# A graph network on one core: GpSimd gathers rows during the recurrent passes, VectorE takes over the low parts, five row buffers, another middle split

## The chip, the core and the metric

The kernel runs on one core of a Trainium2 chip. The metric is the device time of one execution in microseconds; lower is better. The engines are named TensorE (PE, its weight loads PEld), VectorE (DVE), ScalarE (ACT), GpSimd (POOL) and SyncE (SP) as in the profile.

## The reference

Four graph layers follow one another on 6250 nodes of 128 features and 100000 edges, each behind a layer norm and ReLU and with a residual sum. What matters here:

```
edge_index = [src, dst];  agg(h) = segment_sum(h[src], dst, 6250)

x = x + L0(h)   # three times: h = h + agg(h); two dense layers with batch norm and ReLU
x = x + L1(h)   # messages weighed by a sigmoid of source and target scores,
                # summed by target, one GRU step, batch norm over the nodes
x = x + L2(h)   # encoder; then five times:
                #   agg = segment_sum((h @ conv_w[i])[src], dst)
                #   r, z, n gates of a GRU on agg and h; h = (1 - z) * n + z * h
                # then relu, decoder of two dense layers, sigmoid
x = x + L3(h)   # segment_sum(h[src], dst) @ W.T + b
return x
```

## The kernel before

The edges are sorted and turned into a matrix of counts, `count` (6272 by 6272, one byte each) in HBM. Every segment sum is then a dense product of the states with the counts. 6272 rows are 49 blocks (`NB`) of 128. The product is done in thirds of the target columns: per third the whole of 49 blocks `k` is run through, and its sums stand in up to five PSUM banks (`SUMS`). The thirds have 10, 8 and 7 pairs of blocks (`THIRD_PAIRS`), so 2560, 2048 and 1792 columns. A pass over the graph is three thirds, 147 blocks.

`Flow.run` writes out a pipeline over blocks `g` by hand, one program for each engine, tied by semaphores. There are two flows. The first has 8 thirds of plain sums (392 blocks) and an attention part; the second has six layers (18 thirds, 882 blocks): five GRU steps, the last of them with the decoder behind it (`Decode`), and the last graph layer (`Out`). In the second flow third 13, the middle one of layer 4, is blocks 637 to 685, and third 16, the middle one of the last layer, is blocks 784 to 832. For block `g`:

- SyncE loads the counts of the block into one of `row_slots` buffers (9 in the first flow, 6 in the second), once the block that lay there has been widened by both engines. Behind the load may stand four DMAs that put shuffled states of a chunk in place (line 2110).
- VectorE cuts the high part off the state block (`high`, line 2571) and widens the right part of the byte counts to float32r (`wide`, line 2065 is the helper `widen` for both engines). ScalarE makes `hi` of `high` (line 2435) and widens the columns below `BY_ACT[q]`: 1024, 768 and 768 for the three thirds.
- GpSimd subtracts: `lo` = state - `high` (line 2164). For blocks from 3 on this waits until `used` says that TensorE has finished block `g - 3`, thus `used >= g - 2`.
- TensorE multiplies `hi` and `lo` with `wide`, bank by bank (line 2226). It waits for `hi`, `lo` and ScalarE's part, and for VectorE's part only before the first bank that needs it. At the end of a block it counts `used` up. `high`, `hi`, `lo` and `wide` have three buffers each.

The chunks (one or two blocks of finished sums) of the third before are worked off in between, one every four blocks: gate products, sigmoids and tanh, the GRU update on VectorE, the shuffle. Chunks of the decode layer go through a longer chain, at fixed distances in blocks from their start (`CHAIN`): hidden 5, decoded 7, relu 8, biased 10, opened 11, scaled 12, kept 14, bias 17. The first decode chunk starts at block 638, so its inverse root stands at block 650 of GpSimd's program (lines 2127 to 2177, it counts `scaled` up), and its normalization at step 652 of ScalarE's (line 2537):

```
for c in self.due(g - CHAIN["kept"], "decode"):
    u = c.late % 2
    e.wait_ge(s["scaled"], c.late)
```

VectorE waits at chunk `late` for `scaled` of chunk `late - 2`. Every engine's instructions run in the order of its program, so a wait holds all that stands behind it.

The only indirect DMAs before are ten gathers in the sort (line 443), 128 rows of 1536 bytes each.

Of the kernel before, what the change touches and what calls it, by code (L numbers as in the profile page):

```python
# [9 lines left out]
F32 = mybir.dt.float32  # L10
# [6 lines left out]
I32 = mybir.dt.int32  # L17
# [6 lines left out]
D = 128  # L24
# [34 lines left out]
SUMS = [[(128, 384), (512, 512), (1024, 512), (1536, 512), (2048, 512)],  # L59
        [(0, 512), (512, 512), (1024, 512), (1536, 512)],  # L60
        [(0, 512), (512, 512), (1024, 512), (1536, 256)]]
BY_ACT = [1024, 768, 768]
ROW_BYTES = 10 * PAIR
ROW_SLOTS = 9
STEP_ROW_SLOTS = 6
WIDE_SLOTS = 3
CUT_SLOTS = 3
HEAD = 4
# [95 lines left out]
class Count:  # L164


    def __init__(self, engine, sem):
        self.engine, self.sem, self.n = engine, sem, 0
# [1709 lines left out]
class Flow:  # L1878
# [1 line left out]

    def __init__(self, net, layers, add_self=False, enter=None, given=()):
        self.net, self.layers, self.add_self, self.enter, self.given = net, layers, add_self, enter, given
        self.row_slots = ROW_SLOTS if enter is None else STEP_ROW_SLOTS
        self.gated = isinstance(layers[0], Gru)
        self.kinds = ["dense" if isinstance(l, list) else "leave" if isinstance(l, Leave) else "attend" if isinstance(l, Attend) else "out" if isinstance(l, Out) else "decode" if l.after else "gru"
                      for l in layers]
        self.parts = [(n, q) for n, kind in enumerate(self.kinds) for q in (ATTEND_PARTS if kind == "attend" else range(3))
                      if n or q not in given]  # L1890
        self.total = len(self.parts) * NB
        self.plain = sum(self.kinds[n] != "attend" for n, _ in self.parts) * NB
        self.head, self.chunks = [], []
        self.need = [[0] * NB for _ in layers]
        made = moved = self.products = 0
        ahead = 0 if given else HEAD if enter is None else HEAD + ENTER["source"]
        for q in () if given else range(3):
            for b, n in self.chunk_blocks(q):
                made += 1
                at = b - ahead - (enter is not None and b == 0)  # L1900
                self.head.append(Chunk(b, n, -1, -1, at, -made, 0, 0, at + ahead - HEAD, made, 0))
        for third, (n, q) in [(-1, (0, q)) for q in given] + [*enumerate(self.parts)]:
            base, tail = (third + 1) * NB, third + 1 == len(self.parts)
            moves = n + 1 < len(layers) and self.kinds[n] in ("dense", "gru")
            for j, (b, nb) in enumerate(self.chunk_blocks(q)):
                spaced = 2 if tail else LEAVE_EVERY[q] if self.kinds[n] == "leave" else EVERY
                at = base + (TAKE_AT + 1 if tail else 1) + spaced * j
                made += n + 1 < len(layers) and not moves
                moved += moves
                late = 1 + sum(c.layer == n for c in self.chunks)  # L1910
                turn = late if self.kinds[n] == "attend" else len(self.chunks) + 1
                self.chunks.append(Chunk(b, nb, n, third, at, turn, j % 2 if tail else 0, int(tail and j > 0),
                                         at + LAG, made, late, moved if moves else 0))
        self.starting, self.turning = defaultdict(list), defaultdict(list)
        self.moving = defaultdict(list)
        self.shuffled = {}
        for c in self.chunks:
            self.starting[c.at].append(c)
            if c.moved:
                self.moving[c.at + WIDE_SLOTS + 2].append(c)  # L1920
        for c in self.head + self.chunks:
            if c.layer + 1 < len(layers):
                if c.layer < 0:
                    self.turning[c.product].append(c)
                    self.products = c.made
                for b in range(c.first, c.first + c.blocks):
                    if c.moved:
                        self.shuffled[c.layer + 1, b] = c
                    self.need[c.layer + 1][b] = c.late if c.layer >= 0 and self.kinds[c.layer] == "leave" else c.made
        self.entering = {c.at: c for c in self.head} if enter is not None else {}  # L1930
        self.steps = range(-ahead - 2 * (enter is not None), self.chunks[-1].at + LAG + WIDE_SLOTS + 1)
# [49 lines left out]

    def run(self):
        net, nc, ps = self.net, self.net.nc, self.net.ps
        total, plain, gated, layers = self.total, self.plain, self.gated, self.layers
        L = 0 if gated else len(layers[0])
        final = layers[-1].out if self.kinds[-1] == "out" else None
# [9 lines left out]
            "first", "second", "mid", "gates", "rz", "pre", "new", "next", "dve", "gated", "gate", "weighed", "attended",  # L1996
            "hidden", "relu", "decoded", "biased", "opened", "spread", "pool", "scaled", "biases", "last", "done", "store",
            "measured", "power", "factors", "normal", "turned", "added", "seen", "rooted", "even", "back", "plain",
            "coded", "code", "encoded", "entered", "squares", "moved0", "moved1", "w_turned", "w_cut", "w_made", "w_kept", *[f"lv_{n}" for n in LEAVE if leaving]]
        with ExitStack() as tmp, stage(nc, *names) as (block, s):  # L2000
            wide = scratch(nc, tmp, "wide", [P, WIDE_SLOTS, ROW_BYTES], F32R)
            high = scratch(nc, tmp, "high", [P, CUT_SLOTS, P], I32)
# [12 lines left out]
            ring = net.ring[:, :, :].rearrange("p j f -> p (j f)")  # L2015
            rows = ring[:, 0:row_slots * ROW_BYTES].rearrange("p (j f) -> p j f", f=ROW_BYTES)
            if self.enter is not None:
                c0, size = row_slots * ROW_BYTES, self.enter.steps * 3 * D * 4
                combined = ring[:, c0:c0 + size].bitcast(F32).rearrange("p (n g f) -> p n g f", g=3, f=D)
                turned_w = net.aggT[:, 0:self.enter.steps * D]  # L2020

# [22 lines left out]
            def like(tile, layer, k):  # L2044

                return tile.rearrange("p (i b) -> p i b", b=SQUARE) if (layer, k) in self.shuffled else tile
# [13 lines left out]
            def along(row, n):  # L2060
                return row.rearrange("p (a f) -> p a f", a=1).to_broadcast([P, n, P])
# [61 lines left out]
            def _(e):  # L2123
# [9 lines left out]
                for g in self.steps:  # L2133
# [23 lines left out]
                        e.tensor_scalar(m, m, -1.0, None, ALU.mult).then_inc(s["lv_root"], 1)  # L2157
                    if not 0 <= g < plain:
                        continue
                    n, q, k = self.where(g)  # L2160
                    e.wait_ge(s["high"], g + 1)
                    if g >= CUT_SLOTS:
                        e.wait_ge(s["used"], g - CUT_SLOTS + 1)
                    e.tensor_tensor(like(lo[:, g % CUT_SLOTS, :], n, k), piece(n, k), like(high[:, g % CUT_SLOTS, :].bitcast(F32), n, k),  # L2164
                                    ALU.subtract)\
                        .then_inc(s["lo"], 1)
                    for c in self.due(g - CHAIN["scaled"], "decode"):
                        u = c.late % 2
                        mean, var = (mv[u][:, 0:c.blocks, i] for i in (0, 1))
# [8 lines left out]
                    for c in self.due(g - CHAIN["bias"], "decode"):  # L2178
                        e.wait_ge(s["kept"], c.made)
                        x = net.xN[:, c.cols].rearrange("p (b f) -> p b f", f=P)  # L2180
                        e.tensor_tensor(x, x, along(layers[c.layer].after.next_bias, c.blocks), ALU.add).then_inc(s["biases"], 1)

            @block.tensor
            def _(e):
# [364 lines left out]
            def _(e):  # L2549
                ch = Count(e, s["dve"])  # L2550
                for g in self.steps:
# [9 lines left out]
                    if 0 <= g < plain:  # L2561
                        n, q, k = self.where(g)
                        c = self.shuffled.get((n, k))
                        if c is not None and q == 0:
                            e.wait_ge(s[f"moved{c.moved % 2}"], (c.moved + 1) // 2 * SQUARES * 16)
                        elif q == 0 and self.need[n][k]:
                            e.wait_ge(s["kept"], self.need[n][k])
                        if g >= CUT_SLOTS:
                            e.wait_ge(s["hi"], g - CUT_SLOTS + 1)
                            e.wait_ge(s["lo"], g - CUT_SLOTS + 1)  # L2570
                        e.tensor_scalar(like(high[:, g % CUT_SLOTS, :], n, k), piece(n, k, I32), HIGH_BITS, None, ALU.bitwise_and)\  # L2571
                            .then_inc(s["high"], 1)
                        e.wait_ge(s[f"row{g % row_slots}"], g // row_slots * 16 + 16)
                        if g >= WIDE_SLOTS:
                            e.wait_ge(s["used"], g - WIDE_SLOTS + 1)
                        widen(e.tensor_copy, g, BY_ACT[q], THIRD_PAIRS[q][1] * PAIR).then_inc(s["wide_dve"], 1)
                    if g >= NB and g % NB == TAKE_AT and g // NB <= last_third:
                        take(e, g // NB - 1, self.takes(g // NB - 1)[0], "took_dve")

# [116 lines left out]
def program(nc, a, out):  # L2696
# [3 lines left out]
    with ExitStack() as ctx:  # L2700
# [68 lines left out]
        def wt(key):  # L2769
            return [net.wT[:, i, :] for i in names[key]]  # L2770
# [82 lines left out]
        with ExitStack() as room:  # L2853
# [8 lines left out]
            step, decoded = [Gru(wt("2ih"), wt("2hh"), *gru_biases(b2i, b2h, b2s), after=after)  # L2862
                             for after in (None, Decode((wt("2d1")[0], d1[:, :]), (wt("2d2")[0], d2_row[:, :]), b3_row[:, :]))]
            Flow(net, [step] * (steps - 1) + [decoded, Out(wt("3")[0], out)],
                 enter=Enter(states_bn[:, :], gam[:, :], bet[:, :], encoder, w_steps, steps, wt("2ih"))).run()


        flag = nc.values_load(many[0:1, 0:1], min_val=0, max_val=1)
# [35 lines left out]
```

## Time and profile before

| | us |
|---|---|
| median of 2 runs | 4062.59 (4062.26 to 4062.91) |
| profiled execution | 4062.36 |
| its span in the trace | 4060.0 |
| TensorE, VectorE, ScalarE, GpSimd busy | 3727.4, 3118.8, 2452.0, 1336.7 |

The trace's span is 2.4 us shorter than the time of the same execution. The mean granted clock of TensorE was 0.994 of full speed. Time in the trace counts from the span's start; the second flow's blocks run from 1998 to 4046.5 us. A busy TensorE isn't TensorE at its peak, since matmuls overlap. Idle time on an engine that is not the bottleneck costs nothing.

### The profile page before, as it was taken

The page shows a single profiled execution, that of the slowest core. Times are in us where ns is not written, and L with a number is a line of the kernel's source. Part 1 is how long each engine was busy: PE and PEld are TensorE (multiplying, and loading weights), DVE is VectorE, ACT ScalarE, POOL GpSimd, SP SyncE. Part 2 cuts the span into 40 slices and gives each one's busy share as a digit, 9 for nine tenths or more (in the row PEclk, how much of TensorE's full clock was granted, in tenths as well). Part 3 has the DMA queues.
Part 4 walks back from the last instruction along what each step waited for, and adds up shares of the span by engine and source line. Part 5 has one row for each costly group of instructions (what it writes and reads, how often), then busy time and mean ns, then how long its engine had stood idle before and what let it go on. Part 6 is the DMA issues. An engine that isn't in the chain of part 4 may idle for free.

```text
span 4060.0 us, 59938 instructions
## 1 busy us (share of the span) xinstructions
PE 3727.4 (92%) x17068; PEld 2915.6 (72%) x17068; DVE 3118.8 (77%) x5632; ACT 2452.0 (60%) x4604; POOL 1336.7 (33%) x1931
## 2 busy tenths in 40 slices
PE   0138889999999999999899999999999999999999
PEld 0126678888888644555688888888888888888887
DVE  9999956677687777877668767877876876786685
ACT  1129956656656787787565555555565555566655
POOL 0011145534545310000361343244244234446624
PEclk9999999999999999999899999999999999999999
DMA  2029954545543322221144444444444445434344
GB/s 64 0 102 365 364 179 135 160 136 142 160 125 104 92 72 73 74 62 53 59 114 119 123 136 130 122 136 130 123 132 137 119 117 141 122 100 111 116 134 135
DMA packets 320447, 509.08 MB, mean 125 GB/s; under 512 B 118819, under 2 KB 187164, under 8 KB 319735
## 3 DMA queue, kind: packets, MB, share of 16 engines
q1 hardware_dynamic: 299484, 452.24, 39.0%
q0 software_dynamic: 7696, 46.93, 3.2%
q10 hardware_dynamic: 12938, 6.05, 0.7%
q8 instruction: 143, 2.34, 0.2%
q14 instruction: 186, 1.52, 0.1%
HBM read 396.98 MB, written 43.87 MB: 109 GB/s over the span
## 4 chain that ended last, share of the span: by engine, by line
PE 50%; issue 0%; ACT 0%; DVE 0%; POOL 0%; ACTq 0%; POOLq 0%
PE ps L2226 41%; PE ps L2342 3%; PE ps L2343 3%; PE ps L2345 1%; PE ps L2344 1%; PE ps L2372 0%; PE ps L2258 0%; PE ps L2328 0%; PE ps L2367 0%; PE ps L2264 0%; PE ps L2249 0%; ACT wide L2065 0%; PE ps L2241 0%; PE ps L2383 0%; PE ps L2193 0%
## 5 line engine op out<-in xcount | busy, mean ns | idle before, releaser
L2226 PE MATMUL ps<-wide,hi 128*128 128x512 f32 (+2 forms) x5537 | 2148.5, 390 | 21.2 <-issue 9.6
L2226 PE MATMUL ps<-wide,lo 128*128 128x512 f32 (+2 forms) x5537 | 2075.9, 379 | 0.0
L2065 DVE CAST wide<-ring 128x1536 fp32r<-128x1536 uint8 (+2 forms) x1274 | 1310.7, 1029 | 492.4 <-PE ps L2226 487.9
L2226 PEld LDWEIGHTS ps<-wide,hi 128*128 128x128 f32 x5537 | 1041.9, 188 | 226.2 <-issue 31.0
L2226 PEld LDWEIGHTS ps<-wide,lo 128*128 128x128 f32 x5537 | 1043.1, 188 | 189.1
L2065 ACT CAST wide<-ring 128x768 fp32r<-128x768 uint8 (+1 forms) x1274 | 1153.5, 905 | 3.2 <-DMA ring<-count 2.4
L2435 ACT CAST hi<-high 128x128 fp32r<-128x128 f32 x1274 | 381.3, 299 | 1042.8 <-PE ps L2226 621.8
L2164 POOL TENSOR_TENSOR lo<-hN,high 128x128 fp32r<-128x128 f32 x686 | 563.3, 824 | 754.4 <-PE ps L2226 438.6
L2164 POOL TENSOR_TENSOR lo<-hB,high 128x128 fp32r<-128x128 f32 x588 | 495.4, 843 | 751.2 <-PE ps L2226 492.5
L2222 PE MATMUL ps<-hN,hB 128*128 128x512 f32 (+1 forms) x1274 | 526.2, 570 | 5.6 <-DVE aggT L2398 4.2
L2428 ACT ACTIVATE hN<-aggT,source_scores 128x512 f32<-128x512 f32 (+1 forms) x637 | 428.9, 695 | 119.0 <-PE ps L2222 87.8
L2559 DVE TENSOR_TENSOR hN<-hN,ring 128x512 f32<-128x512 f32 (+1 forms) x637 | 402.4, 668 | 110.5 <-ACT hN L2428 105.5
L2222 PEld LDWEIGHTS ps<-hN,hB 128*128 128x128 f32 x1274 | 241.4, 191 | 264.3 <-issue 209.6
L2571 DVE TENSOR_SCALAR high<-hN 128x128 int32<-128x128 int32 x686 | 225.1, 328 | 8.3 <-DVE hB L2686 3.9
L2587 DVE SCALAR_TENSOR_TENSOR room<-ps,b2h,room 128x256 f32<-128x256 f32 (+1 forms) x125 | 59.9, 479 | 204.2 <-ACT room L2456 204.2
L2571 DVE TENSOR_SCALAR high<-hB 128x128 int32<-128x128 int32 x588 | 197.1, 335 | 0.6 <-POOL lo L2164 0.6
L473 PE MATMUL ps<-ident,aggT 128*128 128x128 f32 x112 | 27.5, 427 | 168.4 <-DVE aggT L191 168.4
L686 ACT ACTIVATE aggT<-ps 128x1024 uint16<-128x1024 f32 x196 | 165.6, 846 | 26.4 <-PE ps L634 26.3
L2343 PE MATMUL ps<-hT,wT 128*128 128x256 f32 (+1 forms) x600 | 175.8, 375 | 0.0
L634 PEld LDWEIGHTS ps<-right,left 128*128 128x128 bf16 x1225 | 99.5, 158 | 97.1 <-DVE left L586 49.4
L2127 POOL TENSOR_SCALAR states_bn<-states_bn 128x1 f32<-128x1 f32 x1 | 0.2, 231 | 506.7 <-POOLq L151 506.7
L634 PE MATMUL ps<-right,left 128*128 128x128 bf16 x1225 | 124.6, 242 | 39.2 <-DVE right L588 38.4
(244 smaller groups left out, 3384.6 us busy)
## 6 DMA issues: line engine op xcount, KB each, us to landing
ring<-count SPq DMA_DIRECT2D x490, 320.0 KB, 3.0
ring<-count SPq DMA_DIRECT2D x441, 256.0 KB, 2.7
ring<-count SPq DMA_DIRECT2D x490, 224.0 KB, 2.6
wide<-aggT POOLq DMA_DIRECT2D x49, 896.0 KB, 6.4
count<-aggT SPq DMA_DIRECT2D x49, 800.0 KB, 4.0
hB<-mid SPq DMA_DIRECT2D x192, 32.0 KB, 1.9
hN<-mid SPq DMA_DIRECT2D x192, 32.0 KB, 1.9
hB<-squares SPq DMA_DIRECT2D x96, 32.0 KB, 2.2
```

The lines of the kernel that those rows point to most:

```text
L634: ins = e.matmul(ps[:, bank + t % PER // 4, t % 4 * P:(t % 4 + 1) * P], left[u][:, :, t], right[u][:, :, t, :], start=True, stop=True)
L686: e.activation(rows[k % ROW_BUFFERS][:, t0 * P:t1 * P], ps[:, bank:bank + 2, :].rearrange("p b f -> p (b f)") [:, 0:(t1 - t0) * P], ACT.Co ...
L2065: return copy(wide[:, g % WIDE_SLOTS, c0:c1].rearrange("p (t u f) -> p t u f", u=2, f=P), rows[:, g % row_slots, c0:c1].rearrange("p (t f ...
L2164: e.tensor_tensor(like(lo[:, g % CUT_SLOTS, :], n, k), piece(n, k), like(high[:, g % CUT_SLOTS, :].bitcast(F32), n, k), ALU.subtract)\
L2222: ins = e.matmul(ps[:, c, 0:size], source(n, k), weights(g, c), start=k == 0, stop=k == NB - 1, skip_group_check=True)
L2226: ins = e.matmul(ps[:, c, 0:size], part[:, g % CUT_SLOTS, :], wide[:, g % WIDE_SLOTS, w0:w0 + size], start=k == 0 and part is hi, stop=k = ...
L2342: e.matmul(o, gates_of(c)[g_], net.aggT[:, c.cols], start=True, stop=False)
L2343: e.matmul(o, gru.w_state[g_], net.hT[:, c.cols], start=False, stop=True)
L2428: e.activation(weights(g, c), layers[n].target_scores[:, sums_at(q, c)], ACT.Sigmoid, bias=layers[n].source_scores[:, k:k + 1]).then_inc(s ...
L2435: e.copy(hi[:, g % CUT_SLOTS, :], high[:, g % CUT_SLOTS, :].bitcast(F32)).then_inc(s["hi"], 1)
L2559: e.tensor_tensor(gate, gate, rows[:, g % row_slots, c0:c1].rearrange("p (t f u) -> p t u f", u=2, f=P), ALU.mult).then_inc(s["weighed"], 1)
L2571: e.tensor_scalar(like(high[:, g % CUT_SLOTS, :], n, k), piece(n, k, I32), HIGH_BITS, None, ALU.bitwise_and)\
```

## The change

`lo` goes from GpSimd to VectorE, behind VectorE's widening, in both flows. The middle third's split goes from 768 to 1024 columns for ScalarE. The second flow has five row buffers; the sixth buffer's bytes become four tiles of 128 by 128 float32 and a list of row numbers. In the second flow GpSimd issues, at the first block of each middle third (blocks 49, 196, 343, 490, 637, 784), 144 indirect DMAs of 128 rows of the input `x` (512 bytes each) into the four tiles in turn; all but the first four of a burst add to what is there. Each waits for the one before it on its tile. Nothing reads the tiles. At its end GpSimd's program waits for all of them.

The four hunks after the constants are the buffers, GpSimd's program at block g, its end, and VectorE's program at block g.

```diff
-BY_ACT = [1024, 768, 768]
+BY_ACT = [1024, 1024, 768]
-STEP_ROW_SLOTS = 6
+STEP_ROW_SLOTS = 5
...
             if self.enter is not None:
-                c0, size = row_slots * ROW_BYTES, self.enter.steps * 3 * D * 4
+                c0, size = (row_slots + 1) * ROW_BYTES, self.enter.steps * 3 * D * 4
+                spare = ring[:, row_slots * ROW_BYTES:(row_slots + 1) * ROW_BYTES].bitcast(F32)
+                tiles = spare[:, 0:4 * D].rearrange("p (n f) -> p n f", f=D)
+                names = spare[:, 4 * D:4 * D + 36].bitcast(U32)
...
-                    n, q, k = self.where(g)
-                    e.wait_ge(s["high"], g + 1)
-                    if g >= CUT_SLOTS:
-                        e.wait_ge(s["used"], g - CUT_SLOTS + 1)
-                    e.tensor_tensor(like(lo[:, g % CUT_SLOTS, :], n, k), piece(n, k), like(high[:, g % CUT_SLOTS, :].bitcast(F32), n, k),
-                                    ALU.subtract)\
-                        .then_inc(s["lo"], 1)
+                    if self.enter is not None and g == NB:
+                        e.iota(spare[:, 4 * D:4 * D + 36].bitcast(I32), pattern=[[29, 36]], base=0, channel_multiplier=41).then_inc(s["named"], 1)
+                        e.wait_ge(s["named"], 1)
+                    if self.enter is not None and g % (3 * NB) == NB:
+                        e.wait_ge(s["used"], g - 1)
+                        for i in range(144):
+                            m = 36 * (g // (3 * NB)) + i // 4
+                            if m:
+                                e.wait_ge(s[f"acc{i % 4}"], 16 * m)
+                            if i < 4:
+                                e.indirect_dma_start(out=tiles[:, i % 4, :], out_offset=None, in_=self.x,
+                                                     in_offset=bass.IndirectOffsetOnAxis(ap=names[:, i // 4:i // 4 + 1], axis=0))\
+                                    .then_inc(s[f"acc{i % 4}"], 16)
+                            else:
+                                e.indirect_dma_start(out=tiles[:, i % 4, :], out_offset=None, in_=self.x,
+                                                     in_offset=bass.IndirectOffsetOnAxis(ap=names[:, i // 4:i // 4 + 1], axis=0), compute_op=ALU.add)\
+                                    .then_inc(s[f"acc{i % 4}"], 16)
...
+                if self.enter is not None:
+                    for j in range(4):
+                        e.wait_ge(s[f"acc{j}"], 16 * 36 * (plain // (3 * NB)))
...
                         if g >= CUT_SLOTS:
                             e.wait_ge(s["hi"], g - CUT_SLOTS + 1)
-                            e.wait_ge(s["lo"], g - CUT_SLOTS + 1)
                         e.tensor_scalar(like(high[:, g % CUT_SLOTS, :], n, k), piece(n, k, I32), HIGH_BITS, None, ALU.bitwise_and)\
                             .then_inc(s["high"], 1)
...
                         widen(e.tensor_copy, g, BY_ACT[q], THIRD_PAIRS[q][1] * PAIR).then_inc(s["wide_dve"], 1)
+                        e.wait_ge(s["high"], g + 1)
+                        e.tensor_tensor(like(lo[:, g % CUT_SLOTS, :], n, k), piece(n, k), like(high[:, g % CUT_SLOTS, :].bitcast(F32), n, k),
+                                        ALU.subtract).then_inc(s["lo"], 1)
```

## Rows read from the trace of the kernel before

**Rows 1.** The page's part 1: busy us, share of the span, instructions

```profile
PE 3727.4 (92%) x17068; PEld 2915.6 (72%) x17068; DVE 3118.8 (77%) x5632; ACT 2452.0 (60%) x4604; POOL 1336.7 (33%) x1931
```

**Rows 2.** Busy time by stretches: us, PE, PEld, DVE, ACT, POOL, clock, DMA

```profile
2118.00:2233.00 115.00, 114.98 (x522) 96.24 (x521) 99.13 (x156) 63.56 (x128) 26.00 (x48) 1.00 0.44 120
2233.00:2340.00 107.00, 107.00 (x514) 90.42 (x513) 80.62 (x160) 64.21 (x132) 43.09 (x53) 1.00 0.45 124
...
3597.00:3730.00 133.00, 126.48 (x609) 106.08 (x608) 94.07 (x234) 84.46 (x185) 78.17 (x156) 0.99 0.36 100
...
3865.00:3960.00 95.00, 94.86 (x438) 78.99 (x437) 83.97 (x112) 51.85 (x100) 22.86 (x50) 1.00 0.48 134
3960.00:4046.50 86.50, 86.50 (x439) 73.06 (x438) 55.60 (x109) 52.22 (x101) 46.80 (x49) 1.00 0.49 142
```

**Rows 3.** Groups of instructions by form, 1400 to 4060 us

```profile
L2065 ACT CAST wide<-ring 128x768 fp32r<-128x768 uint8 x588 | 488.6, 831 | 0.4
...
L2065 DVE CAST wide<-ring 128x1280 fp32r<-128x1280 uint8 x294 | 435.7, 1482 | 28.9 <-PE ps L2226 28.6 <-issue 0.3
...
L2065 ACT CAST wide<-ring 128x1024 fp32r<-128x1024 uint8 x294 | 307.5, 1046 | 0.1
...
L2065 DVE CAST wide<-ring 128x1024 fp32r<-128x1024 uint8 x294 | 203.1, 691 | 82.1 <-PE ps L2226 82.0
```

**Rows 4.** Groups by form, VectorE, counting stage (280 to 520 us)

```profile
L602 DVE TENSOR_TENSOR lo<-hN,high 128x128 fp32r<-128x128 f32 x49 | 14.2, 290 | 3.4 <-PE ps L648 3.4
```

**Rows 5.** Timeline of VectorE, middle third of the first recurrent pass

```profile
2184.91 1.48 DVE L2065 CAST wide<-ring 128x1280 fp32r<-128x1280 uint8 x1
2186.30 0.42 DVE L2595 TENSOR_TENSOR hT<-hT,room 128x256 f32<-128x256 f32 x1
```

**Rows 6.** The view of DMA issues: KB each, us to landing

```profile
ring<-count SPq DMA_DIRECT2D x490, 320.0 KB, 3.0
...
hN<-sorted_keys,tile_i POOLq DMA_INDIRECT x10, 3.1
```

**Rows 7.** Timeline of GpSimd, the sort's ten indirect gathers

```profile
252.22 1.26 POOL L443 DMA_INDIRECT hN<-sorted_keys,tile_i  x1 [248.70 <-DVE tiles_before L364]
...
264.21 1.03 POOL L443 DMA_INDIRECT hN<-sorted_keys,tile_i  x1 [0.30 <-issue]
```

**Rows 8.** Timeline of VectorE beside and after those gathers

```profile
256.83 0.42 DVE L393 TENSOR_SCALAR hN<-hN,flip_col 128x384 int32<-128x384 int32 x1 [0.28 <-DMA hN<-sorted_keys,tile_i]
...
266.66 0.41 DVE L393 TENSOR_SCALAR hN<-hN,flip_col 128x384 int32<-128x384 int32 x1
```

**Rows 9.** Line 2164 (lo) by stretches from the flow's start; x counts blocks

```profile
1997.80:3493.70 1495.90, 531.57 (x638) 1.00 0.46 127
...
1997.80:3868.00 1870.20, 633.97 (x785) 1.00 0.44 124
```

**Rows 10.** Timeline of GpSimd, middle third of the decode pass

```profile
3489.47 1.24 POOL L2164 TENSOR_TENSOR lo<-hN,high 128x128 fp32r<-128x128 f32 x1 [0.94 <-PE ps L2226]
...
3493.83 0.46 POOL L2164 TENSOR_TENSOR lo<-hN,high 128x128 fp32r<-128x128 f32 x1 [1.72 <-PE ps L2226]
...
3525.76 0.23 POOL L2127 TENSOR_SCALAR root<-mv 128x1 f32<-128x1 f32 x1 [1.75 <-DVE mv L2657]
...
3528.59 0.36 POOL L2177 TENSOR_SCALAR off<-off 128x1 f32<-128x1 f32 x1
```

**Rows 11.** Timeline of ScalarE, the same stretch

```profile
3529.15 0.83 ACT L2065 CAST wide<-ring 128x768 fp32r<-128x768 uint8 x1
3529.89 0.49 ACT L2537 ACTIVATE hB<-xN,off,inv 128x128 f32<-128x128 f32 x1
...
3537.01 0.30 ACT L2435 CAST hi<-high 128x128 fp32r<-128x128 f32 x1 [0.90 <-DVE high L2571]
```

**Rows 12.** Timeline of GpSimd, middle third of the last layer

```profile
3868.14 0.46 POOL L2164 TENSOR_TENSOR lo<-hB,high 128x128 fp32r<-128x128 f32 x1 [1.72 <-PE ps L2226]
```

**Rows 13.** Timeline of SyncE's queue at the end

```profile
4048.65 4.67 SPq L2084 DMA_DIRECT2D out<-xN  x8
```

More of the change, by code:

```diff
@@ L1878, with __init__ @@
 class Flow:
-    def __init__(self, net, layers, add_self=False, enter=None, given=()):
+    def __init__(self, net, layers, add_self=False, enter=None, given=(), x=None):
+        self.x = x
         self.net, self.layers, self.add_self, self.enter, self.given = net, layers, add_self, enter, given
@@ L1998, in run @@
             "measured", "power", "factors", "normal", "turned", "added", "seen", "rooted", "even", "back", "plain",
-            "coded", "code", "encoded", "entered", "squares", "moved0", "moved1", "w_turned", "w_cut", "w_made", "w_kept", *[f"lv_{n}" for n in LEAVE if leaving]]
+            "coded", "code", "encoded", "entered", "squares", "named", "acc0", "acc1", "acc2", "acc3", "moved0", "moved1", "w_turned", "w_cut", "w_made", "w_kept", *[f"lv_{n}" for n in LEAVE if leaving]]
         with ExitStack() as tmp, stage(nc, *names) as (block, s):
@@ L2864, in program @@
             Flow(net, [step] * (steps - 1) + [decoded, Out(wt("3")[0], out)],
-                 enter=Enter(states_bn[:, :], gam[:, :], bet[:, :], encoder, w_steps, steps, wt("2ih"))).run()
+                 enter=Enter(states_bn[:, :], gam[:, :], bet[:, :], encoder, w_steps, steps, wt("2ih")), x=a["x"]).run()
         flag = nc.values_load(many[0:1, 0:1], min_val=0, max_val=1)
```

## The prediction

> **What bounds the kernel now.** I read the page's totals first, then stretches of the recurrent flow, then single engines. TensorE is busy 92% of the span, GpSimd 33% [rows 1]. In a recurrent pass (49 blocks in each of three thirds) TensorE is busy 114.98 us of 115 and 107.00 of 107 at full clock, VectorE 99 and 81, GpSimd only 26 and 43 [rows 2]: TensorE bounds five of the six passes and nothing that relieves another engine shortens them. The exception is the stretch with the decode chain: 126.48 of 133 us, so 6.5 us of TensorE idle [rows 2]. The two last thirds (3865 to 4046.5) are TensorE-bound again. So I look for what the change can put *in front of* TensorE, and there GpSimd counts for its place in the program, not for its load.
>
> **VectorE and ScalarE part.** In the middle third VectorE widens 1280 columns in 1482 ns, in the last third 1024 columns in 691 ns [rows 3]. The new middle split leaves it 1024 columns, the very form of the last third: 0.79 us less per middle block. ScalarE goes from 768 to 1024 columns, 831 to 1046 ns [rows 3], 0.22 us more; it is busy 63.56 us of 115 there [rows 2], 74 after, so this costs nothing; without that slack it would be 0.22 us for each of 294 blocks. The subtraction for `lo` took 290 ns as a VectorE instruction of the same form in the counting stage [rows 4], so at most 0.29 us per block, in all 1274 blocks. In the middle third VectorE, busy 99 us of 115, comes to 99 - 49 x (0.79 - 0.29) = 75; the start-to-start time of a 1280-column widening, 1.39 us (2184.91 to 2186.30) [rows 5], is no longer most of a block. In the last third it comes to 81 + 49 x 0.29 = 95 us of 107 [rows 2], still below TensorE. `lo` now comes behind the widening, so TensorE can no longer begin a block on ScalarE's columns alone. VectorE works up to three blocks ahead, which hides it; where a flow starts with nothing ahead it costs at most one widening, 1 us for each of two flows. VectorE's wait for GpSimd's `lo` becomes program order. What can be won is the idle of the decode stretch; of the 6.5 us I take 5, between 0 and 6.5.
>
> **Five row buffers.** A load is now asked for five blocks ahead instead of six. Five of the shortest blocks last over 8 us (86.5/49 = 1.77 us each [rows 2]); row loads land in 3 us [rows 6]. Cost nothing; were it to bite it would show as row waits on ScalarE and VectorE.
>
> **The gathers: length of one burst.** 144 indirect DMAs, issued in order by GpSimd, with at most four under way, since each waits for the one four before it. The nearest rows are ten indirect gathers of 128 rows in the sort: first at 252.22, tenth at 264.21, so 1.332 us from one to the next, of which 1.03 is the instruction and 0.30 the gap in the last one [rows 7]. They land 3.1 us after issue [rows 6]; four slots last 5.3 us, so at that landing time issue is the limit, not the chain. A burst is 144 x 1.332 = 192 us. The sort's rows are 1536 B, these 512 B; the number of rows is the same. Bounds: 144 x 1.03 = 148 us with no gap, and upward what accumulation or contention costs (rivals): some 290 us. Rows speak for little contention: VectorE's one-input operation on 384 columns, two results a cycle, lasts 0.42 us under a gather's issue and 0.41 us with none [rows 8], and the 1.332 us of the train already hold such neighbours. But a widening is longer. In the middle third of the last layer (95/49 = 1.94 us a block [rows 2]) it and the cut take 0.60 + 0.13 us from start to start, 38% of the time. I let a quarter of that fall on the gathers, my choice between none and all: 9%, 210 us for the last burst, and 197 us for the fifth, of which only the first 43 us run beside a busy VectorE.
>
> **Where bursts lie.** They stand at blocks 49, 196, 343, 490, 637 and 784, each released when TensorE has finished two blocks before. In the first four GpSimd owes nobody anything: `lo` has moved away, and a pass, 1495.9/638 x 147 = 345 us [rows 9], is longer than a burst. Price nothing.
>
> The fifth is another matter. The 639th `lo` of the flow, which has the same condition as this burst, starts at 3493.83 [rows 9, 10]. Behind it in GpSimd's program stand the decode's inverse roots, the first at block 650, at 3525.76 and done at 3528.8 [rows 10]. ScalarE in its step 652 waits for `scaled` before it goes on to the next block's `hi` and widening; it widened block 652 at 3529.15 and cuts `hi` of 655, which needs TensorE done with 652, at 3537.01 [rows 11]. So ScalarE sticks, and TensorE runs dry at about 3537. It goes on when the burst has been issued, plus 3.1 us for the roots, 0.5 us for the normalization and 1.1 us for `hi` and widening. Stop = 3493.8 + 197 + 4.7 - 3537 = 159 us. None of it is given back: TensorE is the bound behind it. Bounds: 110 us at 148, 252 us at 290.
>
> The sixth burst starts with the `lo` at 3868.14 [rows 9, 12], later by the stop. The block's GpSimd program ends in a wait for all of it. Issue 210, last landing 2, and the 4 us that lie before between the last store's issue and landing and the span's end (store queue busy 4048.65 to 4053.3 [rows 13], landing some 2.5 us later, my estimate from the landings of rows 6): 3868.1 + 210 + 2 + 4 = 4084 against a span of 4060, so 24 us more; 0 at 148 us, 104 at 290.
>
> **Sum.** 4062.4 (the profiled execution, 0.2 us from the median) - 5 + 159 + 24 = 4240 us, +4.4%.
>
> **Rivals.** (1) *Accumulation is slow.* If a gather that adds takes L from issue to landing, a tile's chain sets the burst: 36 x L, which overtakes issue at L = 5.33 us. For it: the adding form isn't in this trace, and every landing here shares the engines with row loads. Against: 3.1 us leaves 2.2 us of room, and a row is a third as long. At L = 8: 288 us, stop 250, tail 102, 4410 us.
>
> (2) *The shared port.* GpSimd's subtraction grows from 0.46 to 1.24 us beside VectorE's widenings [rows 10], so some exclusion exists. If descriptor writing stood still under each fast widening and cut, the sixth burst would be 192/(1-0.38) = 310 us and the fifth 43 + (192 - 27) = 208: stop 170, tail 124, 4351 us. And if VectorE in turn waited out a whole issue (1 us) before its widening and its cut, a middle block would be 3.7 us instead of 2.47: some 60 us for each of five bursts, 4650 us. Rows 8 speak against both. The Trainium skill, "SBUF — State Buffer", section "Who interferes with whom", states such a lock: a VectorE operation in a two-port mode fully blocks GpSimd's descriptor writes, and by that rule the time would be this rival's 4351. The trace agrees for GpSimd's compute instructions and, in ten gathers, shows next to none of it for issue.
>
> (3) *Issue goes by bytes: not slower.* If issuing 512-byte rows took a third of 1.03 us and the gap vanished beside it, a burst were 49 us, the stop 11 and the tail nothing: 4068 us, within 2%. The point is the burst at which the stop passes 81 us, 120 us, or 0.83 us a gather. Against: nothing in the ten gathers ties the issue to the bytes, which land long after it; the list of rows that GpSimd goes through is as long.
>
> (4) *GpSimd does not gate the decode*, because its waits are laid out otherwise than I read, leaving only the tail: 4081 us. Against: the order in the program, and ScalarE's normalization at 3529.89 that follows the roots' end at 3528.95 [rows 10, 11].
>
> **Chances.** Forecast (both terms, bursts of 180 to 230 us) 0.60; slow accumulation 0.18; port lock 0.14; rivals 3 and 4 0.05; anything else slower 0.03. The range goes from bursts of some 150 us (stop 112, 4170) to those of some 300 (4430). A measurement tells 2%, 81 us, from no change: slower 0.94, same 0.05, faster 0.01.
>
> **What would show it.** GpSimd: 864 indirect DMAs at 1.3 to 1.5 us spacing in six trains. TensorE: no loss in passes one to four, which stay as long as before; one hole of some 160 us in the decode pass, ended by ScalarE, itself released by GpSimd's offsets; an end at which only GpSimd works. VectorE's middle widenings at 0.69 us. I am wrong if the hole isn't there, if passes one to four lengthen (port or row buffers), or if spacing is over 1.7 us.

## The result: 7.8% slower, a 229 us stop and a 98 us tail

The changed kernel takes 4379.48 us (2 runs, 4378.09 to 4380.87) against 4062.59 us: ratio 1.078, 95% interval 1.0765 to 1.080. The profiled execution took 4380.87 us, its span in the trace 4376.2 us, 316.2 us more than before. The page's totals (busy us, share of the span, instructions), the chain that ended last by engine, and GpSimd's costliest group (count, busy us, mean ns, idle time before it):

```profile
PE 3724.4 (85%) x17068; PEld 2916.4 (67%) x17068; DVE 2934.5 (67%) x6906; ACT 2523.5 (58%) x4604; POOL 1731.2 (40%) x1522
...
PE 40%; POOL 11%; issue 3%; ACT 1%; DVE 1%; DMA 0%; ACTq 0%; DVEq 0%; POOLq 0%
...
L2179 POOL DMA_INDIRECT ring<-in_x,ring x840 | 1395.6, 1661 | 258.4 <-issue 255.4
```

TensorE does the same 17068 matmuls in the same busy time as before [rows 1], in a longer span. It has no more work; it has more idle time. GpSimd is busy 40% on the page, which is still no bottleneck by load, yet it now holds 11% of the chain that ended last. Where it does so is seen by stretches (us, then busy PE, PEld, DVE, ACT, POOL, clock, DMA share, GB/s):

```profile
2131.00:2471.00 340.00, 339.34 (x1576) 286.62 (x1575) 235.72 (x600) 203.22 (x376) 242.64 (x145) 1.00 0.69 156
...
3151.00:3491.00 340.00, 339.34 (x1576) 286.68 (x1575) 234.86 (x599) 203.69 (x376) 242.62 (x145) 1.00 0.69 156
3491.00:3533.00 42.00, 41.66 (x195) 34.74 (x193) 25.37 (x73) 23.04 (x43) 35.30 (x23) 1.00 0.62 133
3533.00:3763.00 230.00, 1.57 (x4) 1.31 (x5) 0.91 (x3) 2.67 (x6) 189.10 (x130) 0.51 0.29 35
3763.00:3790.00 27.00, 26.95 (x121) 22.11 (x120) 21.02 (x69) 19.66 (x38) 12.41 (x26) 0.95 0.37 103
...
4266.00:4376.00 110.00, 3.64 (x27) 2.96 (x25) 2.98 (x7) 0.00 (x0) 80.67 (x53) 0.54 0.30 41
```

The first four passes, each with a burst in it, cost next to nothing: TensorE is busy 339.3 us of 340. A busy engine need not be one at its peak, so the length counts too: from ScalarE's first `hi` of block 49 to that of block 637 it is 1360.3 us here (2127.9 to 3488.2) and 1359.8 in the kernel without gathers (2126.8 to 3486.6). From 3533 to 3763 TensorE works 1.57 us of 230, and hardly anything but GpSimd is busy; from 4266 to the end the same. The waits of the stretch 3480 to 3800 (engine, tile and line, released by; us in total, times, longest) name both links of the stop:

```profile
ACT hB L2556 <- POOL off L2192: 236.0, 4, 233.8
...
PE ps L2245 <- ACT wide L2070: 228.8, 1, 228.8
```

One wait of 233.8 us for GpSimd's offsets, and behind it one of 228.8 us of TensorE for ScalarE's widening. GpSimd's timeline shows the last gather of the fifth burst and, straight behind it in its program, the roots that the decode was waiting for (start, duration, tile, the idle before it in brackets):

```profile
3755.40 1.54 POOL L2179 DMA_INDIRECT ring<-in_x,ring  x1 [0.30 <-issue]
3757.01 0.25 POOL L2132 TENSOR_SCALAR root<-mv 128x1 f32<-128x1 f32 x1
...
3759.38 0.24 POOL L2192 TENSOR_SCALAR off<-off 128x1 f32<-128x1 f32 x1
```

The six bursts start at 2130.9, 2470.3, 2810.4, 3150.5, 3490.6 and 4086.6 us and last 285.7, 286.3, 286.3, 286.3, 266.4 and 276.0 us, from the first issue to the end of the last. All instructions of the adding gather, and of the plain one with which each tile begins (ns: least, median, most; first and last start), and what GpSimd was idle for ahead of them:

```profile
L2179 POOL DMA_INDIRECT ring<-in_x,ring x840: 1535/1553/2250, 2136.5 to 4361.0; - x168
...
  issue: 255.4, 838
  DMA ring<-in_x,ring: 3.0, 2
```

```profile
L2175 POOL DMA_INDIRECT ring<-in_x,ring x24: 943/1063/1492, 2130.9 to 4091.0; - x24
```

An adding gather takes 1.54 us to issue where nothing else works, a plain one 0.94 at the least and 1.06 in the median, as those of the sort took 1.03 [rows 7]. With the 0.30 us gap the quiet spacing is 1.85 us, not the 1.33 of [rows 7]. Only 2 of 840 waited for a landing.

The account, in the profiled executions: stop +228.8; from the start of TensorE's last matmul of line 2245 (2226 before) to the span's end 111.5 us (4264.7 to 4376.2) against 13.4 (4046.6 to 4060.0), +98.1; all else -10.7. Together +316.2 us of span. The remaining 2.3 us lie between span and execution time (4.7 us against 2.4).

### The profile page after: what moved, and what is told of

Read it like the earlier page. It is cut to its first block, busy times and chain, and to the rows that moved or that the text cites. A ratio compares the mean times of both kernels' runs of the same rounds, so it can differ in the third digit from the quotient of the medians.

```text
span 4376.2 us, 58666 instructions
## 1 busy us (share of the span) xinstructions
PE 3724.4 (85%) x17068; PEld 2916.4 (67%) x17068; DVE 2934.5 (67%) x6906; ACT 2523.5 (58%) x4604; POOL 1731.2 (40%) x1522
## 3 DMA queue, kind: packets, MB, share of 16 engines
q0 software_dynamic: 129424, 103.61, 13.7%
## 4 chain that ended last, share of the span: by engine, by line
PE 40%; POOL 11%; issue 3%; ACT 1%; DVE 1%; DMA 0%; ACTq 0%; DVEq 0%; POOLq 0%
PE ps L2245 32%; POOL ring L2179 10%; PE ps L2361 2%; PE ps L2362 2%; PE ps L2364 1%; PE ps L2363 1%; ACT wide L2070 0%; PE ps L2277 0%; PE ps L2283 0%; DMA ring<-in_x,ring 0%; POOL ring L2175 0%; PE ps L2391 0%; PE ps L2386 0%; POOL inv L2133 0%; PE ps L2268 0%
## 5 line engine op out<-in xcount | busy, mean ns | idle before, releaser
L2179 POOL DMA_INDIRECT ring<-in_x,ring x840 | 1395.6, 1661 | 258.4 <-issue 255.4
L2070 DVE CAST wide<-ring 128x1024 fp32r<-128x1024 uint8 (+1 forms) x1274 | 1029.9, 808 | 607.4 <-PE ps L2245 568.1
L2070 ACT CAST wide<-ring 128x1024 fp32r<-128x1024 uint8 (+1 forms) x1274 | 1237.8, 972 | 4.5 <-DMA ring<-count 3.7
L2132 POOL TENSOR_SCALAR root<-mv 128x2 f32<-128x2 f32 (+1 forms) x75 | 40.0, 534 | 1075.8 <-DVE mv L2700 851.6
L2596 DVE TENSOR_TENSOR lo<-hN,high 128x128 fp32r<-128x128 f32 x686 | 195.2, 285 | 0.0
L2596 DVE TENSOR_TENSOR lo<-hB,high 128x128 fp32r<-128x128 f32 x588 | 166.6, 283 | 0.0
L2556 ACT ACTIVATE hB<-xN,off,inv 128x128 f32<-128x128 f32 x49 | 21.6, 487 | 249.2 <-POOL off L2192 249.0
```

Source lines behind the costliest of these rows:

```text
L2070: return copy(wide[:, g % WIDE_SLOTS, c0:c1].rearrange("p (t u f) -> p t u f", u=2, f=P), rows[:, g % row_slots, c0:c1].rearrange("p (t f ...
L2179: e.indirect_dma_start(out=tiles[:, i % 4, :], out_offset=None, in_=self.x, in_offset=bass.IndirectOffsetOnAxis(ap=names[:, i // 4:i // 4 ...
```

## The experiments

Each kernel is the changed one with the edit shown. "Spacing" is from one gather's start to the next. The kernel before took 4060.65 to 4062.23 us on the chips of these runs; figures with an interval come from three or five rounds, the others from one run. The diffs are cut to the lines that matter. All but the three kernels without gathers and the one with `lo` on GpSimd number their gathers through (`issued`) instead of anew in each burst, so that each tile's wait still counts rightly.

**Without gathers, and the other edits one by one.** What do the edits do that aren't gathers?

```diff
-                    if self.enter is not None and g % (3 * NB) == NB:
-                        e.wait_ge(s["used"], g - 1)
-                        for i in range(144):
...
n_six:  as above, and
-STEP_ROW_SLOTS = 5
+STEP_ROW_SLOTS = 6
n_768:  as above with five buffers, and
-BY_ACT = [1024, 1024, 768]
+BY_ACT = [1024, 768, 768]
```

> No gathers at all; lo on VectorE, middle split at 1024, five buffers stay. In the changed kernel blocks outside the stop ran some 12 us shorter than before (3 us ahead at the first burst, 8 us in the decode pass). If that is the other edits': 4050 us. If the edits cost nothing and gain nothing: 4062.

> As n_all, but six row buffers. If five are as good as six: the same as n_all within 0.1%. If five cost something: faster than n_all.

> As n_all, but the middle third split at 768 again, so VectorE widens 1280 columns in 1.48 us and subtracts too. If the gain of the decode pass comes from the split: 5 to 10 us slower than n_all, and TensorE idle again in the decode's middle third. If the gain comes from lo having left GpSimd: the same as n_all.

Measured: without gathers 4047.72 us, ratio 0.9966 (0.9952 to 0.9979); with six buffers 4046.62 us, 0.9964 (0.9951 to 0.9978); with the old split 4065.38 us, 1.0009 (1.0000 to 1.0018), beside 4061.51 us for the kernel before. So the fifth-buffer edit costs nothing that five rounds can see (1.1 us), the split is worth 17.7 us, and moving `lo` to VectorE without the new split costs some 4. The difference between the two splits was expected to be 5 to 10 us, and to lie in the decode pass; it is larger and spread out. In the profiled executions (15.2 us apart) 2.6 us of it are there where the second flow's first middle third begins, about 1.9 us come in each of the next four passes, 4.8 in the middle third of the decode pass, and next to nothing behind it. That middle third, first without gathers, then with the old split:

```profile
3476.00:3601.00 125.00, 125.00 (x581) 105.24 (x580) 88.33 (x258) 85.24 (x162) 32.24 (x71) 1.00 0.37 104
```

```profile
3487.00:3616.00 129.00, 126.98 (x587) 106.03 (x586) 118.99 (x257) 75.74 (x164) 26.27 (x71) 1.00 0.35 101
```

With the old split VectorE is busy 119 us of 129 there, and TensorE loses 2 us in it. With the new one VectorE is at 88 of 125 and TensorE is never idle.

The gain over the kernel before lies elsewhere: in the last third of the decode pass, where TensorE was idle 6.5 us of 133 [rows 2], and in the third behind it. First without gathers, then with the old split:

```profile
3601.00:3712.00 111.00, 110.12 (x543) 93.41 (x542) 83.16 (x257) 74.77 (x161) 41.79 (x86) 1.00 0.36 101
```

```profile
3616.00:3727.00 111.00, 108.95 (x536) 92.11 (x535) 86.26 (x259) 72.80 (x159) 41.13 (x87) 1.00 0.35 101
```

Measured from ScalarE's first `hi` of a third to that of the next, the last decode third takes 116.4 us in the kernel before, 110.0 without gathers and 109.7 with the old split; the third behind it 132.9, 131.0 and 131.0. These 8 us come with either split, so they are the work of `lo` having left GpSimd. Moving `lo` thus wins some 8 us there and, with the old split, loses more than that in the middle thirds, where VectorE then widens 1280 columns and subtracts too.

The six-buffer version, which drops the unused gathers, beats both kernels by a little, and is the fastest one run.

**Which burst costs what.** One burst left out.

```diff
g_no5:
-                    if self.enter is not None and g % (3 * NB) == NB:
+                    if self.enter is not None and g % (3 * NB) == NB and g != 13 * NB:
g_no6:  the same with g != 16 * NB
```

> The fifth burst (block 637) is left out, five remain. If the stop of 229 us is its doing alone: 4379 - 229 = 4150 us, tail of 98 us still there. If bursts cost everywhere: about 4330.

> The sixth burst (block 784) is left out. If the tail is its doing: 4379 - 98 = 4281 us, the stop of 229 us still there, and the span ends some 7 us after the last store as before. If part of the quiet 13.7 us after the last gather belongs to GpSimd's waits at the end, those go too.

Measured: 4144.98 us without the fifth, 4281.15 us without the sixth. The stop belongs to the one burst, the tail to the other: without the fifth TensorE is busy throughout the stretch in which it stood still.

```profile
3480.00:3610.00 130.00, 130.00 (x605) 109.36 (x604) 91.99 (x272) 90.02 (x172) 35.98 (x80) 1.00 0.39 105
```

Without the sixth the span ends at 4276.8 us, 6.9 us behind the store queue's last entry (4265.20 + 4.67), as it ended 6.7 us behind it before [rows 13]. With the sixth it ends 13.7 us behind the last gather's issue (4360.98 + 1.54 = 4362.5). Of these, eight pass with no DMA traffic at all:

```profile
4362.50:4364.00 1.50, 0.00 (x0) 0.00 (x0) 0.00 (x0) 0.00 (x0) 0.02 (x1) 0.50 0.36 44
4364.00:4372.00 8.00, 0.00 (x0) 0.00 (x0) 0.00 (x0) 0.00 (x0) 0.00 (x0) 0.50 0.00 0
4372.00:4376.00 4.00, 0.00 (x0) 0.00 (x0) 0.00 (x0) 0.00 (x0) 0.00 (x0) 0.50 0.04 12
```

**Half a burst.** Is the stop the burst less a constant?

```diff
-                        for i in range(144):
...
+                        for i in range(72):
```

> 72 gathers per burst instead of 144 (half of the added work is left out). If the stop is the burst's length less 38 us and the tail its length less 178 us: burst 133 us, stop 95, no tail: about 4145 us. If a burst costs TensorE in proportion: half of the 317 us, 4220 us.

Measured: 4148.17 us. The fifth burst lasted 133.5 us and TensorE's one wait was

```profile
PE ps L2244 <- ACT wide L2070: 95.9, 1, 95.9
```

133.5 - 95.9 = 37.6; with 144 gathers 266.4 - 228.8 = 37.6. The stop is burst minus 37.6 us at both lengths. The total is 4148 us, as the first of the two expectations had it (4145). There is no tail: the sixth burst ends before the last layer does.

**Is it the landing?** 36 adding gathers on a single tile, so each waits for the one before it to land.

```diff
-                        for i in range(144):
-                            m = 36 * (g // (3 * NB)) + i // 4
...
+                        for i in range(36):
+                            t, m = issued[0] % 1, issued[0] // 1
...
+                            kind = {} if i < 1 else dict(compute_op=ALU.add)
```

> 36 gathers per burst, all on one tile, so each waits for the landing of the one before: spacing is the time L from issue to landing of an adding gather. If L is about that of the plain gathers in the sort (3.1 us plus the longer issue, 3.6): burst 130 us, stop 92, no tail, 4142 us. If accumulation is slow (L over 7.4, where a chain on four tiles would overtake issue): burst over 266, 4380 us or more.

Measured: 4145.54 us. GpSimd's timeline during the stop:

```profile
3562.22 1.54 POOL L2177 DMA_INDIRECT ring<-in_x,ring  x1 [2.01 <-DMA ring<-in_x,ring]
3565.71 1.54 POOL L2177 DMA_INDIRECT ring<-in_x,ring  x1 [1.95 <-DMA ring<-in_x,ring]
```

So the landing comes some 3.5 us after the issue's start, and 4.0 to 4.5 us (the median of a burst) where the other engines work. Four slots of 1.85 us last 7.4 us. The landing doesn't set the pace of the four-tile burst, and the fifth burst is 132.8 us with a stop of 95.1, again 37.7 apart.

**Is it the bytes?** Rows of 128 bytes in place of 512, still adding.

```diff
-                                e.indirect_dma_start(out=tiles[:, i % 4, :], out_offset=None, in_=self.x,
...
+                            e.indirect_dma_start(out=tiles[:, t, 0:32], out_offset=None, in_=self.x.rearrange("n (h f) -> (n h) f", h=4),
```

`x` is taken here as four times as many rows of 32 columns, and the same list of row numbers picks from them.

> Each gather adds 32 columns (128 bytes) per row instead of 128; as many rows and gathers, other values summed. If issue goes by rows: spacing 1.85, about 4380 us. If it goes by bytes (rival 3 of the prediction): well under 1 us spacing, stop near 100 us or less, under 4170 us.

Measured: 4377.97 us, the same as with full rows, and the issue is the same too (this line's median holds the 24 plain ones):

```profile
L2177 POOL DMA_INDIRECT ring<-in_x,ring x864: 944/1545/2262, 2130.1 to 4358.4; - x173
```

The issue doesn't go by bytes: a quarter of them changes nothing.

**Is it the adding?** All gathers plain, on the same four tiles.

```diff
-                            if i < 4:
...
+                            kind = {} if True else dict(compute_op=ALU.add)
```

> All 864 gathers plain, none adds (the tiles are overwritten, which nothing reads). In the changed kernel an adding gather takes GpSimd 1.55 us plus a gap of 0.30, a plain one 1.06. If the adding form is what made a burst 266 to 286 us instead of 192, spacing falls to 1.36 us, the fifth burst to 196 us, the stop to 159, the tail to some 30: about 4240 us. If the longer issue comes from the row traffic, the port or the waits in the flow, spacing stays at 1.85 and the time at 4380.

Measured: 5068.05 us, ratio 1.2482 (1.2461 to 1.2503), a miss in the total and a hit in the term it was made for. The issue is

```profile
L2177 POOL DMA_INDIRECT ring<-in_x,ring x864: 940/944/1479, 2131.1 to 4885.0; - x173
```

so spacing 1.25 us and bursts of 181 to 183 us, about what the sort's gathers gave me (192). The time went elsewhere. Without gathers the same kernel takes 4047.72 us, so a burst costs 170 us in the mean (1020 us over six). The first burst, plain gathers first, the changed kernel second:

```profile
2131.00:2312.00 181.00, 47.88 (x147) 32.02 (x145) 18.19 (x50) 17.37 (x31) 137.32 (x144) 0.57 0.27 71
```

```profile
2131.00:2312.00 181.00, 180.89 (x837) 152.04 (x836) 126.69 (x341) 111.14 (x212) 152.66 (x94) 1.00 0.71 153
```

TensorE works a quarter of the burst, and the DMA engines are *less* busy, 0.27 against 0.71. Two of the waits in that stretch ("remote" is a release that the profile puts down to no engine of this core, such as a landing):

```profile
ACT hi L2453 <- remote: 108.8, 6, 21.6
DVE wide L2070 <- remote: 105.8, 6, 21.4
```

SyncE's queue issued 12 row loads there in place of 79, each issue still taking 0.33 us. That number alone proves nothing, since a load is asked for only when a block has been widened, and fewer blocks passed. The queues (packets, MB, share of 16 engines), plain first, then the changed kernel:

```profile
q0 software_dynamic: 4551, 9.34, 19.6%
q1 hardware_dynamic: 2977, 3.51, 6.9%
```

```profile
q1 hardware_dynamic: 20519, 21.45, 43.2%
q0 software_dynamic: 12800, 6.04, 27.1%
```

Late row loads would explain VectorE's wait, but they aren't all of it. In TensorE's program `lo`'s matmul of a bank stands right behind that of `hi`, with no wait between them. Over the whole span TensorE was nevertheless idle 72.5 us ahead of `lo` matmuls, against none in the changed kernel (plain first; both from the page):

```profile
L2244 PE MATMUL ps<-wide,lo 128*128 128x512 f32 (+2 forms) x5537 | 2112.7, 385 | 72.5 <-issue 72.5
```

```profile
L2245 PE MATMUL ps<-wide,lo 128*128 128x512 f32 (+2 forms) x5537 | 2075.9, 379 | 0.0
```

So under a train of plain gathers at 1.25 us spacing the row loads seem to come late though the DMA engines have room, and TensorE is held up by something else as well, which no run names; under adding ones at 1.85 us neither happens. Plain gathers differ in two things, the spacing and the packets (4096 bytes, 16 to a gather, against 512 bytes, 128 to a gather). Which of the two does it was not separated and stays open.

**`lo` back on GpSimd, ahead of the bursts.** Does moving `lo` off GpSimd save anything here?

```diff
+                    n, q, k = self.where(g)
+                    e.wait_ge(s["high"], g + 1)
+                    if g >= CUT_SLOTS:
+                        e.wait_ge(s["used"], g - CUT_SLOTS + 1)
+                    e.tensor_tensor(like(lo[:, g % CUT_SLOTS, :], n, k), piece(n, k), like(high[:, g % CUT_SLOTS, :].bitcast(F32), n, k),
+                                    ALU.subtract)\
+                        .then_inc(s["lo"], 1)
                     if self.enter is not None and g == NB:
...
+                            e.wait_ge(s["lo"], g - CUT_SLOTS + 1)
...
-                        e.wait_ge(s["high"], g + 1)
-                        e.tensor_tensor(like(lo[:, g % CUT_SLOTS, :], n, k), piece(n, k), like(high[:, g % CUT_SLOTS, :].bitcast(F32), n, k),
-                                        ALU.subtract).then_inc(s["lo"], 1)
```

> The subtraction for lo goes back to GpSimd, ahead of the bursts in its program; all else as in the changed kernel. If a burst costs what stands behind it on GpSimd: each of six bursts now stops TensorE for its length less a few us, some 264 us each, no tail: about 4062 + 6 x 264 = 5650 us. If moving lo has nothing to do with it: 4380.

Measured: 5636.22 us, against 5650 expected, with six stops of some 261 us. The stretch of the first burst and the waits:

```profile
2140.00:2395.00 255.00, 0.00 (x0) 0.00 (x0) 0.00 (x0) 0.00 (x0) 212.92 (x139) 0.50 0.30 37
```

```profile
PE ps L2252 <- issue: 1573.3, 14, 261.0
DVE high L2597 <- POOL lo L2169: 1561.8, 11, 260.2
```

With everybody waiting for GpSimd all bursts last 263.5 to 263.8 us at 1.84 us spacing. This is the quiet length of a burst. Moving `lo` is what makes four of six bursts free.

**The same 864 gathers spread over the blocks.**

```diff
g_spread:
+   if self.enter is not None and g >= 9:
+       for i in range(min(864 - issued[0], 1 + (g % 5 == 0) if g < 13 * NB else (g + 1) % 2)):
g_spread2:
+   if self.enter is not None and g >= 40:
+       for i in range((0 if g < 40 or issued[0] >= 864 else
+                 (1 + (g % 3 == 0) if g // NB % 3 == 0 else 1 + (g % 7 == 0) if g // NB % 3 == 1 else 1) if g < 13 * NB else
+                 g % 2 if g < 16 * NB else 1)):
```

> All 864 gathers, but issued one or two per block from block 9 on and one per two blocks from block 637 on, so GpSimd is never more than a few us behind. If the cost is the place of the bursts in GpSimd's program: as n_all, 4050 us, both stop and tail gone. If gathers cost through port or memory traffic: the more, the more of the 317 us stays.

> All 864 gathers again, spread so that GpSimd keeps up: none before block 40 (where it still makes inverse roots for the encoder), 4 per 3, 8 per 7 and 1 per block in the three thirds of a pass, one per two blocks in and behind the decode pass, one per block in the last two thirds. In g_spread GpSimd was 15 us late at the start and some 68 us behind when the decode's first root was due. If the cost is what stands behind late gathers: within 15 us of n_all's 4048 us, plus up to 15 us at the end (98 gathers of 2 us against 181 us of blocks), 4050 to 4080 us. If gathers cost in themselves: as g_spread, 4130.

Measured: 4131.02 us, 1.0173 (1.0159 to 1.0187), and 4077.49 us, 1.0040 (1.0027 to 1.0054). The first missed: it lost some 15 us at the flow's start, where GpSimd still makes roots for the encoder, and it fell further behind in the passes: the gather of block 650, behind which the first root stands, was issued at 3592.2, 59 us after ScalarE had cut `hi` of that block (3532.9). GpSimd's backlog then stood as one block of work ahead of the roots, like a small burst:

```profile
ACT hB L2555 <- POOL off L2191: 97.9, 25, 57.1
...
PE ps L2244 <- ACT wide L2070: 57.1, 8, 52.4
```

The second begins later and gives GpSimd about what it can issue: 170 gathers in a pass of 340 us, at the 1.99 us of a live burst. That leaves nothing to catch up with, and at block 637 it was still 38 us behind (3525.0 against 3487.0). Its waits from 3480 to 3700 us:

```profile
ACT hB L2557 <- POOL off L2193: 27.6, 14, 16.0
...
PE ps L2246 <- ACT wide L2070: 11.0, 1, 11.0
```

The same gathers cost some 30 us over the version without them, in place of 332. Part of the 30 is this backlog in front of the roots, so it isn't the price of gathers as such, and no run shows how low it would go with some room in each pass.

## Why the prediction was right, and which term was off

The direction, the mechanism and the two places were right; the time, 4379 against 4240, lay in the upper part of the range. The bursts of 266 and 276 us lay outside the 180 to 230 to which I had given 0.60. The range held them because its upper end, bursts of 300 us, was drawn for another mechanism, slow accumulation; that the time fell inside is in so far luck.

- *Passes one to four free*: shown. TensorE is busy 339.3 of 340 us.
- *The fifth burst stops the decode, and the order in GpSimd's program is why*: shown, by the two waits above, by the run without that burst, and by half a burst. My constant was 38.5 us; three runs with two lengths of burst give 37.6 to 37.7. With the measured burst of 266.4 in it the step gives 228 us against 228.8 measured. Rival 4 is out.
- *Length of a burst, 197 us*: this is the term that was mis-sized. The burst was 266.4 us, the error of the stop (159 against 228.8) is all here. I took 1.03 us of issue from plain gathers [rows 7] and noted that the adding form wasn't in the trace, but looked for its price in the landing (rival 1) rather than in the issue. The runs show 1.54 us for adding and 0.94 for plain with nothing else changed; my 192 us and 144 x (1.54 - 1.03) = 73 more make 265. My own condition for being wrong, a spacing over 1.7 us, was met.
- *A quarter of the overlap, 9%, on gathers beside a busy VectorE*: about right. Live bursts last 286.3 us against 263.6 with every engine still, 8.6%. In the first burst the gathers of about 1.5 us overlapped a VectorE widening for 0.41 us on average and those near 2.0 us for 1.13 us. That it is the widening is argued from this, not shown by a run.
- *The tail, burst less 186*: measured 276.0 gives 90 by that step, against 98.1. The rest, 8 us, is the quiet at the end. I had 2 + 4 = 6 us from the last issue to the end, and it was 13.7. So the end behind the last gather was sized from stores and is twice as long behind gathers. In the version spread over the blocks, which also ends in gathers, it was 12.6 us; without the sixth burst 6.9. Its cause is open.
- *The other edits, 5 us*: 14 (4061.51 to 4047.72). I had looked for the gain in the idle time of the decode stretch alone, and 8 us of it do lie there and in the third behind it, from the moved `lo`. The rest I had put at nothing: some 5 us were won before the second flow's first middle third, and the new split keeps the moved `lo` from costing about 2 us in each pass. VectorE's `lo` lasts 0.28 us [rows 4], its widening of 1024 columns in the second flow 0.73 on average, instead of 1.48 for 1280 [rows 3].
- *Five row buffers, nothing*: shown.

In the port rival I took a middle block as 2.47 us; rows 2 give 115/49 = 2.35, which changes that rival's 4650 us by at most some 30 and decides nothing. Slow accumulation was wrong as a mechanism: the landing would decide from 7.4 us on (four slots of 1.85), and it is 3.5 to 4.5. That its 4410 us is nearer to the result than 4240 is chance. The port lock fails: with descriptor writing halted under each widening, a burst of 1.85 us gathers would be 266/(1 - 0.38) = 430 us, and live ones took 286. By the rule of the Trainium skill, "SBUF — State Buffer", section "Who interferes with whom", a VectorE operation in a two-port mode blocks GpSimd's descriptor writes outright. In this case's trace a burst is longer by 8.6% with VectorE busy 236 us of 340, so the trace doesn't bear the rule out for the whole of an issue. Issue by bytes is out by the narrow rows.

## What to carry to other kernels

Price work put on an idle engine by what stands behind it in that engine's program, up to the next instruction that somebody waits for: burst length minus the slack there (37.6 us here), and nothing wherever no such instruction follows. If the work has to be done, hand it out per block at less than the engine can issue there, starting after its own backlog. Here a schedule just at that limit took 332 us down to 30 and was still 38 us behind at the decode; one that falls further behind is a burst again. And take the duration of an instruction from its own form: an adding gather isn't a plain one, and if the form isn't in the trace, the issue needs a bound of its own as much as the landing.

## What the runs showed of the hardware

- An indirect DMA of 128 rows holds GpSimd for 0.94 us, with accumulation for 1.54 us, with a gap of 0.30 us behind either; 128-byte and 512-byte rows cost the same. An adding one lands about 3.5 us after its issue begins on a quiet core.
- Under a train of plain gathers at 1.25 us spacing TensorE worked 48 us of 181, the DMA engines' share fell from 0.71 to 0.27, and TensorE idled even between two matmuls with no wait between them (72.5 us over the span, against none). The plain gathers, which do less, made the kernel 16% slower than the adding ones did (5068 against 4379 us). The cause is open.
- In the stop the granted clock was 0.51 of full speed, the lower level, 1.2 of 2.4 GHz, and TensorE began again in it: 0.63 us for a matmul every 0.43 us until about 3766, then 0.40 us every 0.23. A stop of 229 us costs only some 2 us more for that:

```profile
3761.99 0.63 PE L2245 MATMUL ps<-wide,lo 128*128 128x512 f32 x1
...
3766.26 0.40 PE L2245 MATMUL ps<-wide,lo 128*128 128x512 f32 x1
```

- A program whose last work is gathers on GpSimd's queue ended 12.6 to 13.7 us behind the last issue, eight of them with no traffic; one that ends in stores 6.7 to 6.9 us behind the store queue's last entry.
